# A graph-attention kernel: VectorE's order of work within a step, and where its edge search runs

## The reference, cut to what matters

```python
h = x @ w_lin + b_lin
msg = h[edge_src]
dense = zeros((n, 32, d)).at[edge_dst, pos].set(msg, mode='drop')   # up to 32 edges of a node
mask  = zeros((n, 32), bool).at[edge_dst, pos].set(True, mode='drop')
xb = _mab(dense, dense, enc..., mask)      # q, k, v; softmax over 32 slots; h = o + x; h + relu(h @ ff_w + ff_b)
xp = relu(xb @ pma_lin_w + pma_lin_b)
p  = _mab(seed, xp, pma..., mask)          # one query for each node
dd = _mab(p, p, dec...)                    # one slot: its softmax is 1
x  = layernorm(x + relu(nan_to_num(dd)))
```

## Time and profile before

| | |
|---|---|
| median of 3 runs | 4447.55 us (4446.77 to 4464.01) |
| the profiled execution | 4459.52 us, of it 4457.7 us between first and last instruction |
| TensorE | busy 73% |
| VectorE | busy 68% |
| GpSimd | busy 69% |
| ScalarE | busy 37% |
| TensorE's mean granted clock | 0.845 |
| the 16 DMA engines, share in the loop | 0.29 |

### The profile page before, as it was taken

How to read it: one execution, slowest core, us unless ns; L and a number is a source line. 1 busy time by engine, 2 the same in 40 slices (tenths; PEclk the granted TensorE clock), 3 DMA queues, 4 the chain that set the end, 5 groups by cost and what they waited for, 6 DMA issues and landing times.

```text
span 4457.7 us, 87178 instructions
## 1 busy us (share of the span) xinstructions
PE 3270.3 (73%) x30724; PEld 2035.1 (46%) x30724; DVE 3038.5 (68%) x7088; ACT 1656.4 (37%) x2990; POOL 3060.7 (69%) x3236
## 2 busy tenths in 40 slices
PE   4777777777777777777777676777776767777777
PEld 3444444444444444444444454544444545444444
DVE  5667676767666667676666676766666667666776
ACT  2334333433333334343333343433333333333433
POOL 3777776767677667676676676766766767667771
PEclk7888888888888888888888888888888888888888
DMA  5333332222222222222232222222222222222330
GB/s 192 84 87 87 85 87 81 81 81 82 78 80 82 78 79 81 78 82 79 78 83 77 82 79 78 82 81 79 82 78 82 78 78 82 78 80 81 90 96 19
DMA packets 170667, 368.55 MB, mean 83 GB/s; under 512 B 56189, under 2 KB 109093, under 8 KB 170229
## 3 DMA queue, kind: packets, MB, share of 16 engines
q0 software_dynamic: 158032, 342.73, 27.9%
q1 hardware_dynamic: 11877, 19.76, 1.2%
q10 hardware_dynamic: 320, 0.10, 0.0%
HBM read 349.58 MB, written 16.32 MB: 82 GB/s over the span
## 4 chain that ended last, share of the span: by engine, by line
PE 47%; DVE 27%; issue 20%; POOL 4%; DVEq 1%; ACT 0%; DMA 0%; SPq 0%; ACTq 0%; POOLq 0%
PE ps L695 10%; PE ps L722 6%; PE ps L637 6%; PE ps L738 5%; PE ps L649 5%; DVE windows L951 5%; PE ps L681 4%; PE ps L708 4%; POOL gathered L545 4%; DVE xb L1090 3%; DVE h L1060 3%; DVE top L1097 2%; DVE total L1047 2%; PE ps L673 2%; DVE flags L906 2%
## 5 line engine op out<-in xcount | busy, mean ns | idle before, releaser
L545 POOL DMA_INDIRECT gathered<-node_table,idx x3125 | 2963.1, 948 | 1217.7 <-issue 894.1
L695 PE MATMUL ps<-h,ff_diag 128*128 128x512 f32 x782 | 506.1, 734 | 551.7 <-DVE h L1060 551.7
L759 ACT ACTIVATE h_apart<-ps 64x512 f32<-64x512 f32 x782 | 462.2, 591 | 989.3 <-PE ps L637 979.7
L1090 DVE SCALAR_TENSOR_TENSOR xb<-ps,cols,h 128x512 f32<-128x512 f32 x391 | 293.7, 751 | 671.9 <-PE ps L695 671.9
L637 PEld LDWEIGHTS ps<-ident,gathered 128*128 128x128 f32 x3128 | 481.2, 203 | 395.5 <-issue 395.5
L637 PE MATMUL ps<-ident,gathered 128*128 128x128 f32 x3128 | 575.3, 312 | 66.2 <-DMA gathered<-node_table,idx 66.1
L1171 DVE STREAM_TRANSPOSE probs_diag<-probs 32x512 f32<-32x512 f32 x784 | 548.9, 700 | 18.3
L722 PE MATMUL ps<-xb,pma_diag 128*128 128x512 f32 x782 | 524.5, 758 | 26.8 <-DVE xb L1090 20.6
L649 PE MATMUL ps<-probs_diag,gathered 128*64 128x128 f32 x6256 | 457.6, 290 | 91.2 <-issue 85.7
L649 PEld LDWEIGHTS ps<-probs_diag,gathered 128*64 128x64 f32 x6256 | 370.2, 169 | 264.6 <-issue 242.6
L814 ACT ACTIVATE xp<-ps,cols 128x512 f32<-128x512 f32 x391 | 267.2, 683 | 513.3 <-PE ps L722 513.2
(11 more groups left out here) (195 smaller groups left out, 3564.1 us busy)
## 6 DMA issues: line engine op xcount, KB each, us to landing
gathered<-node_table,idx POOLq DMA_INDIRECT x3125
node_table<-gathered SPq DMA_DIRECT2D x24, 384.0 KB, 2.6
out_rows<-rows SPq DMA_DIRECT2D x5, 416.0 KB
win_table<-in_dst SPq DMA_DIRECT2D x1, 1716.0 KB
win_table<-in_src SPq DMA_DIRECT2D x1, 1716.0 KB
windows<-win_table,win_idx POOLq DMA_INDIRECT x94
rows<-in_x SPq DMA_DIRECT2D x2, 640.0 KB, 5.2
rows<-in_x SPq DMA_DIRECT2D x1, 768.0 KB, 7.1
```

The source lines that it names most:

```text
L545: pool.indirect_dma_start(out=gathered[:, s.slot(0, RING), t * ROW:(t + 1) * ROW], out_offset=None, in_=table, in_offset=bass.IndirectOffs ...
L695: pe.matmul(ps[:, B_FF, :], ff_diag[:, :], h2[:, s.slot(L_FF, 2), :], start=True, stop=True).then_inc(ff_ps, 1)
L759: return nc.scalar.activation(o, i, ACT.Copy)
L1090: V.scalar_tensor_tensor(xb[:, s.slot(L_FF, 2), :], ps[:, B_FF, :], c_("ff_b", P), h2[:, s.slot(L_FF, 2), :], ALU.add, ALU.max).then_inc(x ...
```

## The change

Four moves in VectorE's program; no other engine's program is changed, and no arithmetic is added or dropped.

- `y_rows` is cut in two. Its addition (L1193) moves from behind the transposes to the very start of step 3, the statistics (L1196) stay behind the transposes.
- In steps 0 and 2, maximum and difference move from behind xb to between h2 and xb. In steps 1 and 3, two of the four transposes do so; the other two stay behind xb.
- The search is cut in two. Counting and the first three shifts (of 256, 128 and 64) stay in step 2 (AT_SEARCH = -6). The other six shifts (32 to 1) and the transpose to `idx` go to the end of step 0, two steps later (AT_SHIFT = -4), with the wait for the gathers that still read the old list.
- `rows_of` moves from step 0 to step 1, one step later (AT_ROWS = -15).

```diff
+AT_SHIFT = -4
-AT_ROWS = -16
+AT_ROWS = -15
+    SHIFTS = 6
             def search(u, h, buffer, at):
+                count_edges(u, h, buffer)
+                shift(u, buffer, range(BITS - 1, SHIFTS - 1, -1))
+                shift(u, buffer, range(SHIFTS - 1, -1, -1))
+                index_of(buffer, at)
+
+            def count_edges(u, h, buffer):
                 dst_win = windows[:, buffer, 0:WIN]
...
-                for b in reversed(range(BITS)):
+
+            def shift(u, buffer, bits):
+                src_win = windows[:, buffer, WIN:2 * WIN + DEG]
+                for b in bits:
                     far = min((1 << b) - 1, WIN - (1 << b)) + DEG
                     V.copy_predicated(src_win[:, 0:far], below_bits[:, b:b + 1].broadcast_to((P, far)),
                                       src_win[:, 1 << b:(1 << b) + far]).then_inc(shifted, 1)
                     wait_apart(dve, shifted, u * BITS + (BITS - b), dve_passed)
+
+            def index_of(buffer, at):
+                src_win = windows[:, buffer, WIN:2 * WIN + DEG]
                 V.transpose(idx[:, at, :], src_win[:, 0:DEG]).then_inc(idx_ready, 1)
...
             def step(s):
+                if s.has_iteration(L_Y):
+                    y_rows(s)
                 if s.has_batch(L_SOFTMAX):
...
                     V.scalar_tensor_tensor(h2[:, s.slot(L_H2, 2), :], ps[:, B_AV, :], c_("bo1", P),
                                            hT[:, s.slot(L_H2, RING), :], ALU.add, ALU.add).then_inc(h2_sb, 1)
+                if s.has_batch(L_SOFTMAX):
+                    n = s.batch(L_SOFTMAX)
+                    dve.wait_ge(s_sb, n + 1)
+                    V.tensor_reduce(top[:, :].rearrange("p (h t) -> p h t", h=2), ps_slots, AX_X, ALU.max
+                                    ).then_inc(s_top, 1)
+                if s.has_batch(L_SOFTMAX):
+                    dve.wait_ge(s_top, n + 1)
+                    V.tensor_tensor(ps_slots, ps_slots,
+                                    top[:, :].rearrange("p (h t) -> p h t", h=2).unsqueeze(3).broadcast_to(
+                                        (P, 2, OCT, DEG)), ALU.subtract).then_inc(s_diff, 1)
+                if s.has_batch(L_NORM):
+                    dve.wait_ge(p_norm, n + 1)
+                    wait(dve, av_ps, s.octet(L_NORM + 2))
+                    to_diagonal(s, pr, 0, QUADS // 2)
...
-                if s.has_batch(L_SOFTMAX):
-                    n = s.batch(L_SOFTMAX)
-                    dve.wait_ge(s_sb, n + 1)
...
                 if s.has_batch(L_NORM):
-                    dve.wait_ge(p_norm, n + 1)
-                    wait(dve, av_ps, s.octet(L_NORM + 2))
-                    to_diagonal(s, pr, 0, QUADS)
+                    to_diagonal(s, pr, QUADS // 2, QUADS)
                 if s.has_iteration(L_Y):
-                    y_rows(s)
+                    y_stats(s)
...
                 if s.has_iteration(AT_SEARCH) and (s.looped or s.at >= 8 + AT_SEARCH):
                     u = s.iteration(AT_SEARCH)
-                    for lag in (10, 9, 8, 7):
+                    par = s.slot(AT_SEARCH, RING) // OCTS_PER_IT
+                    landed(par, s.round(AT_SEARCH))
+                    count_edges(u, par, par)
+                    shift(u, par, range(BITS - 1, SHIFTS - 1, -1))
+                if s.has_iteration(AT_SHIFT) and (s.looped or s.at >= 8 + AT_SHIFT):
+                    par = s.slot(AT_SHIFT, RING) // OCTS_PER_IT
+                    shift(s.iteration(AT_SHIFT), par, range(SHIFTS - 1, -1, -1))
+                    for lag in (12, 11, 10, 9):
                         if s.has(lag):
                             dve.wait_ge(g_in[s.slot(lag, RING)], s.round(lag) * (16 * OCT) + 16 * OCT)
-                    par = s.slot(AT_SEARCH, RING) // OCTS_PER_IT
-                    landed(par, s.round(AT_SEARCH))
-                    search(u, par, par, s.slot(AT_SEARCH, PERIOD) // OCTS_PER_IT)
+                    index_of(par, s.slot(AT_SHIFT, PERIOD) // OCTS_PER_IT)
```

More of the change, by code:

```diff
@@ L929, in search @@
             def search(u, h, buffer, at):
+                count_edges(u, h, buffer)
[3 more added lines that the diff above has]
+            def count_edges(u, h, buffer):
                 dst_win = windows[:, buffer, 0:WIN]
-                src_win = windows[:, buffer, WIN:2 * WIN + DEG]
                 node = node_f[:, bass.ds(u, 1)]
@@ L1093, in step @@
                     norm_scale(part)
-                if s.has_batch(L_SOFTMAX):
-                    n = s.batch(L_SOFTMAX)
-                    dve.wait_ge(s_sb, n + 1)
-                    V.tensor_reduce(top[:, :].rearrange("p (h t) -> p h t", h=2), ps_slots, AX_X, ALU.max
-                                    ).then_inc(s_top, 1)
-                if s.has_batch(L_SOFTMAX):
-                    dve.wait_ge(s_top, n + 1)
-                    V.tensor_tensor(ps_slots, ps_slots,
-                                    top[:, :].rearrange("p (h t) -> p h t", h=2).unsqueeze(3).broadcast_to(
-                                        (P, 2, OCT, DEG)), ALU.subtract).then_inc(s_diff, 1)
                 if s.has_batch(L_NORM):
-                    dve.wait_ge(p_norm, n + 1)
-                    wait(dve, av_ps, s.octet(L_NORM + 2))
-                    to_diagonal(s, pr, 0, QUADS)
+                    to_diagonal(s, pr, QUADS // 2, QUADS)
                 if s.has_iteration(L_Y):
-                    y_rows(s)
+                    y_stats(s)
                 if s.has_iteration(L_MASK2):
@@ L1194, in y_rows, with y_stats @@
                                        ).then_inc(y_ok, 1)
+            def y_stats(s):
+                m = s.iteration(L_Y)
+                row = rows[:, bass.ds(m, 1), :].rearrange("p m d -> p (m d)")
                 dve.wait_ge(y_ok, m + 1)
```

## The result

The changed kernel takes **4168.43 us** (median of 4 runs, 4167.17 to 4176.05), the kernel before 4448.81 us in the same comparison (4446.77 to 4464.01). The ratio is 0.9366, with the 95% interval 0.9343 to 0.939: 6.3% faster. The profiled execution took 4176.05 us, of it 4174.2 between first and last instruction.

A forecast was written before the change was run, and what follows sets the result against it. GpSimd's gather issue was to become the bound: last gather at 4101 us, plus 2 for landing, 62 to the end, 2 for TensorE's lateness, makes 4167; with 1.8 from span to execution, 4168 us. Range 4155 to 4190.

The forecast's parts named there:

- step 3: One of an iteration's four steps: predicted to shrink from 14.5 us to between 8.4 and 11.6.
- step 1: One of an iteration's four steps: predicted to grow from 8.0 to 10.1 us, 0.4 for transposes and 1.7 for `rows_of`.
- The bound changes to GpSimd: In the loop, GpSimd's issue of gathers, 41.35 us an iteration, takes over the pace; iterations lasted 44.6 us before.
- The sum: Whole run: last gather at 4101, landing 2, remainder to the end 62, TensorE's lateness 2, span to execution 1.8: 4168 us.
- The step lengths: TensorE's and VectorE's four steps together 35.3 to 38.5 us, with the loop's edge 36.4 to 39.6, against GpSimd's 41.35.
- `y_ok`: Ahead of L708 in step 3: its "issue" is a 3.16 us wait for the rows' addition, 305.5 us in all, and goes.
- A: Loop: only part of the gain arrives, from the rows' addition or the search's move alone; 4200 or 4290 us; chance 0.08.
- B: VectorE's xb comes later while TensorE alone sets the pace: 1.0 us more an iteration, 4555 us; chance 0.04.
- Rival C: TensorE's new waits for rows drop it to the low clock in two of four steps: about 4235 us; chance 0.05.
- Rival D: GpSimd's gathers stretch beside a denser VectorE, say 5% of 0.95 us: +150 us, 4320 us; chance 0.03.
- The moved lists: GpSimd's `idx` written at the end of step 4u - 4 instead of 4u - 6, and `rows_of` one step later: no cost.
- Rival E: The lists come too late for GpSimd and give back the rest's gain: no change, 4455 us; chance 0.03.

The follow-up runs named there:

- E5: The changed kernel with only 6 of the 8 gathers of each octet, the missing rows left out of the computation: 3598.95 us, ratio 0.8091.
- E7: The changed kernel with two tiles of every fourth octet gathered in halves, 196 more gathers in all: 4410.15 us, ratio 0.9921 to the kernel before.
- E1: The kernel before with only the rows' addition moved to the start of step 3: 5630.62 us beside 5616.33, ratio 1.0026.
- E9: The same kernel as E1 (only the rows' addition moved), run again on another chip and occasion: 5567.61 us beside 5564.9, ratio 1.0003.
- E4: The kernel before with only 6 of the 8 gathers of each octet: 4944.41 us beside 5616.33, ratio 0.8802.
- E3: The kernel before with only maximum, difference and two of the four transposes moved between h2 and xb: 5640.24 us beside 5616.33, ratio 1.0038.
- E8: The changed kernel with the second half of the search another two steps later (AT_SHIFT = -2): 4168.5 us, ratio 0.9372 to the kernel before.
- E11: The changed kernel with the search whole again in step 2 and `rows_of` back in step 0: 5582.21 us beside 5568.0 for the kernel before, ratio 1.0022.
- E12: The changed kernel, unaltered, run again where the kernel before takes 5562.51 us: 6343.77 us, ratio 1.1401.

## Why the prediction was right, point by point

**The bound changes to GpSimd: right, at the level it was made for.** The waits, the chain, E5 and E7 show it independently.

**The sum.** It put the last gather's end at 4101; it was 4109.4. The start came 1.6 us later than before, and a gather took (4108.43 - 67.8) / 3220 = 1.2549 us in place of 1.253, which makes 6. The turn of the last octet,

```profile
4114.65 0.72 PE L639 MATMUL ps<-ident,gathered 128*128 128x128 f32 x4
```

is 5.3 us behind that, where 4 were given. From it to the end are 59.6 us, where 62 were given. Together 4174.2 for 4167: the profiled execution lies 8 us over the forecast, and that the median lies on it to half a microsecond is partly luck. The number holds because a queue that never stops needs only its pitch and its count.

**The step lengths: mis-sized, without effect.** 36.4 to 39.6 us were predicted for an iteration of TensorE and VectorE; E5 shows 35.85, under the lower end. E5's own expectation of 3850 us took 38 us from that range and missed by 251, of which 94 x (38 - 35.85) = 202. The mean steps of E5 are 9.0 us (step 3, 8.4 to 11.6 predicted), 9.4 (step 0, 8.5 and the 1.1 of the loop's edge), 8.7 (step 1, 10.1) and 8.7 (step 2, 8.3). So the upper end was wrong in step 3, whose 9 us behind h2 were taken at the low clock; once the waits are gone, the clock is not low. What lies below the lower end is step 1, where 2.1 us were added for `rows_of` and the transposes and 0.7 came. E5's mean clock is 0.956. The stretches of steps 3 and 0 in the changed kernel are

```profile
2007.90:2019.04 11.14, 7.36 (x94) 3.69 (x93) 7.88 (x13) 3.17 (x6) 8.52 (x9) 0.85 0.39 103
...
2019.04:2029.59 10.55, 7.86 (x65) 5.21 (x61) 6.74 (x18) 4.87 (x10) 7.83 (x9) 1.00 0.28 77
```

against 0.53 in step 3 of the earlier trace rows. The cost taken from rows at the low clock didn't survive the removal of the idle time ahead of them.

**`y_ok`: right.** The "issue" wait of L708 was the wait for the rows' addition. It is gone in the changed kernel, and in E1 and E9 too, where that is the only edit, while E4, which has the old order at the same level, keeps 305.6 us of it in 95 times. E3, which moves two of the four transposes out of its way, keeps 180.7. But in E1 its removal gave no time.

**Rivals A and B: refuted at the lower level.** A wanted a wait for h2 or ahead of L708 that remains; 29.7 us and 0.4 remain. B wanted xb to come late; VectorE still waits 640 us for L697 in the whole run, so what stands ahead of xb is covered.

**Rival C, the clock: its mechanism exists, its price doesn't.** Where TensorE stood 3.78 us for rows, the two products of L697 took 1.92 us at the low clock, 0.9 more than the 1.02 they take at the full one in the next step. The Trainium skill's section "HAM oscillation — how this bites in real kernels" of "TensorE: Matmul & The Clock Gate" says that a loop whose turns each wait for a transfer falls back to the low clock at each turn. The trace agrees for this wait, but not for each: in the next step the turn waits 1.81 us for rows, and the clock of that stretch is 1.00. The mean clock rose to 0.912, where the rival wanted less than 0.84. The slow products cost nothing here, because TensorE has 41.38 - 35.85 = 5.5 us to spare in an iteration.

**Rival D, stretched gathers: refuted.** The mean of a gather is 950 ns with VectorE busy 73% and 948 with 84% (E5).

**The moved lists, "neither costs anything": right at the lower level, wrong at the upper.** In the changed kernel at the lower level GpSimd never waits for the list, with 22.3 us to spare, and even E8's 3.6 us are enough. My worry in E8 was wrong because I let VectorE's step 4u - 2 begin only when octet 4u - 2 has landed, and the list come 8 to 10 us later. In E8's trace that step begins at 2036.88, before the octet's last gather ends at 2038.66, and the list is there at 2045.39, 6.7 us behind that gather and not 10 to 12. At the upper level GpSimd is ahead, since TensorE is slow. It does stand for the list, 14.9 us an iteration. The prediction saw this case ("GpSimd may stand and wait for the list, but it then has steps 1 to 3") and judged it by whether the rows still land in time. They do. It missed that at the upper level TensorE slows down beside gathers, so that *when* they are issued matters, not only *by when*. The trace it was made from couldn't show it: there a batch beside gathers takes 1.1 us. Rival E had the right place, but its price was at most the gain given back (4455); at the upper level the loss is 781 us.

## What to carry to other kernels

Where an engine's waits say "idle" but its instructions never pause by more than a fixed gap, count pitch times instructions: that sum gave this result to 0.2%, while all estimates of the other engines' steps were off by more and didn't matter. Adding a little work to the supposed bound, before and after, tests it best: 196 gathers cost 15 us in one kernel and 242 in the other. And measure a change on more than one occasion and chip before keeping it: this one is 6% faster at one level of the machine and 14% slower at the other, and by E11 the loss at the upper level comes from the split search or the `rows_of` that moved with it.

## What the runs showed of the hardware that was not expected

- One kernel, unchanged, ran at 4449 to 4451 us in two comparisons (one of them on the chip numbered 4) and at 5563 to 5616 in four (chips 0, 8, 4 and 14). Within a comparison it never changed.
- The difference sits in TensorE's batches of 64 small products beside GpSimd's gathers: 1.1 us against 4.8 to 19.3. The waits have no releaser in the profile, and the traces at the upper level lack two thirds or more of the semaphore steps of the landings (25 to 35% are there, against 92 to 95%).
- At the same level, ScalarE goes on over 1 us behind TensorE's modelled end in half of the cases beside gathers (47 of 94 in E12) and in none of the others, against 0.04 us in the median at the lower level.
- GpSimd's gather has a pitch of 1.25 us whatever VectorE does, at both levels; the median of one is 946 to 949 ns everywhere.
